# First attention, second half of the tokens: weights reloaded from DRAM as their stored high and low parts

## What is computed

```python
def _L0_xattn_ref(latents, context, Wq, Wk, Wv, Wo):
    H, KV, HD = (16, 4, 96)
    G = H // KV
    hidden = jnp.concatenate([context, latents], axis=1)
    q = (latents @ Wq.T).reshape(b, q_len, H, HD)
    k = (hidden @ Wk.T).reshape(b, s_len, KV, HD)
    v = (hidden @ Wv.T).reshape(b, s_len, KV, HD)
    ...
    attn = jax.nn.softmax(scores.astype(jnp.float32), axis=-1).astype(q.dtype)
    out = jnp.einsum('bkgqs,bksd->bkgqd', attn, v)
    return out @ Wo.T

x = x + _L0_xattn_ref(_layernorm(x, axis=-1), ctx_4096, ...)
x = x + _L0_ffn_ref(_layernorm(x, axis=-1), ...)
...
x = x + _L3_ffn_ref(_layernorm(x, axis=-1), L3_ffn_w1, L3_ffn_w2, L3_ffn_w3)
```

## Time and profile before

| | |
|---|---|
| median of 3 runs | 1762.42 us (1760.4 to 1762.99) |
| profiled execution | 1756.28 us |
| span of its trace | 1754.6 us |
| busy share PE, DVE, ACT, POOL | 83%, 64%, 26%, 18% |
| mean granted clock | 0.884 |
| read from and written to DRAM | 84.34 MB, 10.82 MB |

### The profile page before, as it was taken

How to read it: one execution, slowest core, us unless ns; L and a number is a source line. 1 busy time by engine, 2 the same in 40 slices (tenths; PEclk the granted TensorE clock), 3 DMA queues, 4 the chain that set the end, 5 groups by cost and what they waited for, 6 DMA issues and landing times.

```text
span 1754.6 us, 19242 instructions
## 1 busy us (share of the span) xinstructions
PE 1447.6 (83%) x6585; PEld 1148.8 (65%) x6585; DVE 1126.1 (64%) x2623; ACT 460.9 (26%) x994; POOL 312.5 (18%) x186
## 2 busy tenths in 40 slices
PE   6559999998999889898376878589997576589998
PEld 5337777775766668686265667377875465477786
DVE  4567777767767658767966656734466788854142
ACT  3223433433333323232212113113212322222010
POOL 4101211221112112111121013115422322012120
PEclk9889999999999989899655897569998778799999
DMA  5421331322223221331011012001111000001011
GB/s 187 152 70 51 89 87 49 97 72 72 69 66 84 65 61 42 84 82 41 24 43 38 25 49 90 17 1 36 52 46 48 24 1 1 0 24 61 13 38 48
DMA packets 99410, 96.43 MB, mean 55 GB/s; under 512 B 13138, under 2 KB 72418, under 8 KB 99314
## 3 DMA queue, kind: packets, MB, share of 16 engines
q1 hardware_dynamic: 98802, 94.35, 18.3%
q0 software_dynamic: 512, 0.85, 0.2%
HBM read 84.34 MB, written 10.82 MB: 54 GB/s over the span
## 4 chain that ended last, share of the span: by engine, by line
PE 62%; DVE 26%; issue 4%; ACT 4%; DMA 2%; SPq 1%; POOL 1%; DVEq 0%; ACTq 0%; POOLq 0%
PE bank L1651 48%; PE bank L1991 5%; PE bank L1743 4%; DVE nf_y L1595 3%; DVE st L1136 2%; DVE xn L1154 2%; PE bank L1676 1%; DMA nf_a<-in_L_w 1%; DVE mx L1504 1%; DVE e L1518 1%; PE bank L1733 1%; DVE sm L1516 1%; DVE xT L1113 1%; DVE mx L1187 1%; PE bank L1947 1%
## 5 line engine op out<-in xcount | busy, mean ns | idle before, releaser
L1651 PE MATMUL bank<-xT,slots 128*128 128x512 f32 (+1 forms) x1920 | 462.7, 399 | 9.7 <-DVE xT L1113 6.3
L808 POOL TENSOR_TENSOR slots<-staging,slots 128x1024 fp32r<-128x1024 f32 (+4 forms) x97 | 230.3, 2377 | 1112.3 <-ACT slots L896 1112.2
L1651 PEld LDWEIGHTS bank<-xT,slots 128*128 128x128 f32 (+1 forms) x1920 | 351.9, 184 | 107.7 <-issue 9.4
L1595 DVE TENSOR_SCALAR nf_y<-nf_w 128x512 fp32r<-128x512 f32 (+2 forms) x495 | 233.8, 499 | 25.3 <-PE bank L1991 24.3
L1651 PE MATMUL bank<-slots,h 128*128 128x512 f32 (+1 forms) x728 | 181.6, 410 | 20.1 <-DVE h L1243 13.9
L1651 PEld LDWEIGHTS bank<-slots,h 128*128 128x128 f32 (+1 forms) x728 | 142.9, 197 | 56.8 <-DVE h L1243 14.8
L1991 PE MATMUL bank<-nf_y,nf_d 128*128 128x512 f32 (+2 forms) x495 | 168.8, 425 | 11.3 <-DVE nf_y L1595 9.0
L896 ACT ACTIVATE slots<-staging 128x1024 fp32r<-128x1024 f32 (+4 forms) x97 | 98.1, 1018 | 187.8 <-PE bank L1651 173.7
L929 ACT ACTIVATE e<-bank,mx 128x320 f32<-128x320 f32 x128 | 66.3, 523 | 274.3 <-DVE mx L1190 270.3
L1209 DVE TENSOR_TENSOR x<-bank,x 128x512 f32<-128x512 f32 x72 | 49.7, 691 | 125.0 <-PE bank L1651 125.0
L1991 PEld LDWEIGHTS bank<-nf_y,nf_d 128*128 128x128 f32 (+1 forms) x495 | 94.2, 195 | 47.6 <-DVE nf_y L1595 16.9
(11 more groups left out here) (244 smaller groups left out, 1942.7 us busy)
## 6 DMA issues: line engine op xcount, KB each, us to landing
staging<-in_L_wqkT SPq DMA_DIRECT2D x16, 480.0 KB, 3.6
nf_out<-nf_w SPq DMA_DIRECT2D x30, 256.0 KB, 2.1
staging<-nf_out SPq DMA_DIRECT2D x30, 256.0 KB, 2.8
staging<-in_L_woT SPq DMA_DIRECT2D x16, 384.0 KB, 3.5
staging<-in_L_w SPq DMA_DIRECT2D x12, 512.0 KB, 4.0
nf_a<-nf_max SPq DMA_DIRECT2D x40, 128.0 KB, 3.6
nf_r<-nf_rcp SPq DMA_DIRECT2D x40, 128.0 KB, 3.5
nf_w<-in_L_w SPq DMA_DIRECT2D x15, 256.0 KB, 4.1
```

What stands on the lines that cost most here:

```text
L808: g.tensor_tensor(lo, split_source(i), hi.bitcast(FP32), ALU.subtract).then_inc(*sig.mark("weight_low", i))
L1595: v.tensor_scalar(nf_y[0:rows, i % STAIR_RING, 0:size], w_, bound, first, compare, ALU.mult)\
L1651: ins = mm(dst, l_, r_, start=i == 0, stop=i == len(passes) - 1)
```

## The change

`chunk` gets an argument `again`, the name of the first-half chunk with the same weights; the 18 second-half chunks carry it. For each of the 18 first-half chunks there is a DRAM tensor `saved`. After SP issues the load of the next but one staged chunk it also issues a DMA of the chunk's high and low parts from the ring slot to DRAM (960 KB for qk0, 768 KB for v0 and o0), after waiting for the save two before. A second-half chunk is no longer loaded to `staging` nor split by ACT and POOL. At the step where its split stood, SP waits for the slot to be free, for the save and for the reload two before, and issues one DMA of 960 or 768 KB from DRAM to the slot; PE waits for that DMA. The staging halves alternate over the staged chunks alone. A split into a slot whose former chunk was saved also waits for that save.

```diff
+        def chunk(name, p, dims, loads, dest=None, after=None, again=None):
...
+            if again is not None:
+                first_split[name] = again
+                saved[again] = dram(f"saved{len(saved)}", (p, 2, int(np.prod(dims))))
...
                 chunk(("v0", hf, i), P, (2, G0 * HD0), [((slice(None),), by_k(a["L0_wvT"], 2 * i, 2 * i + 2))],
                      again=("v0", 0, i) if hf else None)
...
+                      again=("qk0", s - G0, i) if s >= G0 else None)
...
+                      again=("o0", s - G0, i) if s >= G0 else None)
...
+            staged = [i for i in range(n_chunks) if chunks[i][0] not in first_split]
+            staged_before = {i: staged[n - 2] for n, i in enumerate(staged) if n >= 2}
...
                 for j in splits_here:
-                    while loads_here and loads_here[0] < j + 2:
+                    if chunks[j][0] in first_split:
+                        steps.append(("reload", j))
+                        continue
+                    while loads_here and (loads_here[0] <= j or staged_before.get(loads_here[0], -1) < j):
                         steps.append(("load", loads_here.pop(0)))
                     steps.append(("split", j))
...
+        def slot_free(engine, name):
+
+
+            n = slot_no[name]
+            if n >= NSLOT and known:
+                former = ring_names[n - NSLOT]
+                engine.wait_ge(*sig.when(*known.user["chunk", former]))
+                if former in saved:
+                    engine.wait_ge(*sig.when(f"weight_saved{save_no[former] % 2}", save_no[former]))
...
+                if n >= 2 and stage_names[n - 2] in saved:
+                    save_chunk(stage_names[n - 2])
+
+            def save_chunk(name):
+
+
+                _, p, dims, *_ = chunks[chunk_no[name]]
+                n = save_no[name]
+                if n >= 2:
+                    sp.wait_ge(*sig.when(f"weight_saved{n % 2}", n - 2))
+                sp.dma_start(saved[name], slots[0:p, slot_no[name] % NSLOT, :, 0:int(np.prod(dims))].bitcast(FP32))\
+                    .then_inc(*sig.mark(f"weight_saved{n % 2}", n, 16))
+
+            def reload_chunk(i):
+                name, p, dims, *_ = chunks[i]
+                n, k = reload_no[name], save_no[first_split[name]]
+                slot_free(sp, name)
+                sp.wait_ge(*sig.when(f"weight_saved{k % 2}", k))
+                if n >= 2:
+                    sp.wait_ge(*sig.when(f"weight_reloaded{n % 2}", n - 2))
+                sp.dma_start(slots[0:p, slot_no[name] % NSLOT, :, 0:int(np.prod(dims))].bitcast(FP32), saved[first_split[name]])\
+                    .then_inc(*sig.mark(f"weight_reloaded{n % 2}", n, 16))
...
             def split(i):
                 name, p, dims, loads, dest, after = chunks[i]
-                act.wait_ge(*sig.when(f"weight_staged{i % 2}", i))
-                if dest is None and slot_no[name] >= NSLOT and known:
-
-                    act.wait_ge(*sig.when(*known.user[("chunk", ring_names[slot_no[name] - NSLOT])]))
+                act.wait_ge(*sig.when(f"weight_staged{stage_no[name] % 2}", i))
+                if dest is None:
+                    slot_free(act, name)
...
             def need(name, user):
 
-                if known:
+                if known and name in first_split:
+                    n = reload_no[name]
+                    pe.wait_ge(*sig.when(f"weight_reloaded{n % 2}", n))
+                elif known:
                     pe.wait_ge(*sig.when("weight_low", chunk_no[name]))
```

More of the change, by code:

```diff
@@ L471, in build @@
         nf_out = [dram(f"nf_out{m}", (FT, P, D)) for m in range(3)]
-        chunks, chunk_no = [], {}
-        def chunk(name, p, dims, loads, dest=None, after=None):
+        chunks, chunk_no, first_split, saved = [], {}, {}, {}
+        def chunk(name, p, dims, loads, dest=None, after=None, again=None):
             chunk_no[name] = len(chunks)
             chunks.append((name, p, dims, loads, dest, after))
+            if again is not None:
+                first_split[name] = again
+                saved[again] = dram(f"saved{len(saved)}", (p, 2, int(np.prod(dims))))
         def by_k(ap, k0_, k1_):
@@ L495, in o0_chunks @@
                 rows = a["L0_woT"][(s % G0 * HPG + 2 * i) * HD0:(s % G0 * HPG + 2 * i + 2) * HD0]
-                chunk(("o0", s, i), HD0, (2, D), [((slice(None),), rows.rearrange("(h p) n -> p h n", p=HD0))])
+                chunk(("o0", s, i), HD0, (2, D), [((slice(None),), rows.rearrange("(h p) n -> p h n", p=HD0))],
+                      again=("o0", s - G0, i) if s >= G0 else None)
         v0_chunks(0)
@@ L643, in build @@
             n_chunks = len(chunks)
-            steps = [(kind, i) for i in range(n_chunks) for kind in ("load", "split")] + base
+            steps = [(kind, i) for i in range(n_chunks)
+                     for kind in (("reload",) if chunks[i][0] in first_split else ("load", "split"))] + base
         slot_no, n = {}, 0
@@ L651, in build @@
         ring_names = sorted(slot_no, key=slot_no.get)
+        stage_no = {n: i for i, n in enumerate(n for n in (c_[0] for c_ in chunks) if n not in first_split)}
+        stage_names = list(stage_no)
+        save_no = {n: i for i, n in enumerate(n for n in stage_names if n in saved)}
+        reload_no = {n: i for i, n in enumerate(n for n in (c_[0] for c_ in chunks) if n in first_split)}
+        def slot_free(engine, name):
[5 more added lines that the diff above has]
+                    engine.wait_ge(*sig.when(f"weight_saved{save_no[former] % 2}", save_no[former]))
         def flat(ap, dims):
@@ L775, in _ @@
                     load_chunk(*s[1:])
+                elif s[0] == "reload":
+                    reload_chunk(*s[1:])
                 elif s[0] == "nf_max":
@@ L785, in split_source @@
         def split_source(i):
-            _, p, dims, *_ = chunks[i]
-            return flat(staging[0:p, i % 2, 0:int(np.prod(dims))], dims)
+            name, p, dims, *_ = chunks[i]
+            return flat(staging[0:p, stage_no[name] % 2, 0:int(np.prod(dims))], dims)
         @block.gpsimd
@@ L2005, in _ @@
             for s in steps:
-                if s[0] in ("load", "split"):
+                if s[0] in ("load", "split", "reload"):
                     continue
```

20 lines of the change are left out of this document (12 added, 8 removed).

## The result

The changed kernel takes 1770.67 us (median of 6 runs, 1766.32 to 1774.25), the kernel before on the same chips 1762.74 us (6 runs, 1760.4 to 1766.63). The ratio is 1.0043 with a 95% interval of 1.0026 to 1.0060: slower, by some 8 us. The profiled execution took 1770.52 us with a span of 1768.7 us. The forecast was 1757.4 us and a gain of 5 us, so it had the wrong sign.

What follows compares the result with a forecast made beforehand. PE was taken as limited by POOL's work through DVE at the joints and by the DMA queue at the start. -16.4 + 10.35 + 1 = -5.05 us on 1762.42 gave 1757.4 us, range 1747 to 1769.

Steps and rivals of the forecast that it cites:

- Joints: Where stages meet: gain of 16.4 us, from closed PE gaps 11.9, the clock 3 and SP's freed waits 1.5.
- DVE's wait at an item's scales: At 580.8 us, 4.63 us behind SP's wait for an o0 split; gain counted 1.5 us, between 0 and 2.2.
- Start: Saves ahead of awaited row blocks on the DMA queue: loss of 10.35 us, bounds 5 and 16, passed whole to PE.
- four qk0 saves: Between 28 and 48 us: 11 us of transfers, less idle queue time, counted as a loss of 5.7 us.
- o0 saves ahead of the block awaited till 61.36 us: At the start: one o0 save of 2.2 us ahead of DVE's row block, 1.9 us of it lost.
- qk0 save ahead of the block awaited till 78.03 us: At the start: one save of 2.75 us ahead of DVE's row block, lost in full.
- the queue's idle time: Between 28 and 48 us: 3.9 us idle, set against 11 us of transfers, leaving 7.1 us.
- My upper bound: At the start: 16 us if all saves from 28 us on are paid in full (4 x 2.75 + 2.2 + 2.75).
- Middle: Rest of the first half: ten saves ahead of background stores and item loads, loss of 1 us, between 0 and 4.
- Reloads: Second-half chunks from DRAM: none late, 0 us, up to 2; tightest place had 14.7 us for 4.2 us.
- The first one: At the start, saves on the single DMA queue cost up to 20 us: +5 to +8 us, about 1769; chance 0.23.

Runs made afterwards that it cites:

- reloads alone: Changed kernel with all 18 reloads but only two chunks saved, which all reloads read (mostly wrong weights); 1750.24 us, ratio 0.9925 to the kernel before.
- POOL's part cut: Kernel before, with POOL's subtraction for the 18 second splits cut to the last 64, 192 or 256 columns; 1749.59 us, ratio 0.9916.
- saves alone: Changed kernel with the 18 saves issued, but second-half chunks loaded and split as before and nothing reloaded; 1785.7 us, ratio 1.0136 to the kernel before.
- fourteen: Changed kernel, saves behind four more row blocks, four early qk0 chunks not saved but split twice; 1755.86 us, ratio 0.9964 to the kernel before.
- eighteen saves put off: Changed kernel, each save behind four more row blocks or the next weight load, reload or turned block; 1753.73 us, ratio 0.9956 to the kernel before.
- nine saves: Changed kernel, only the nine chunks first split after 120 us saved and reloaded, the others split twice; 1763.16 us, ratio 1.0005 to the kernel before.

## Why the prediction was wrong

**Joints (forecast -16.4 us): right, perhaps a little high.** The seven gaps closed, in total -17.6 us by the offsets of one trace, -12 to -16 by the medians of the runs with reloads alone, with POOL's part cut, and of the changed kernel against the saves alone. One of the three terms was not there: DVE's wait at an item's scales, counted at 1.5 us, is 4.20 us instead of 4.63, and PE's gap behind it 2.94 instead of 2.18. What stands before those scales is the same in both kernels: SP needs some 12 us to issue the twenty small DMAs of that item (567.16 to 579.21 us before, 574.05 to 585.76 after). The cause of the gaps, POOL through DVE, is shown by cutting POOL's work alone.

**Start (forecast +10.35, bounds 5 to 16): the first step that failed, by size.** It is 16.8 us in the changed kernel's trace, 14.1 with the saves alone, whose steps at the start are the same. Its three terms, from the offsets of DVE's maxima at 48.73, 61.36 and 78.03 us before:

| term | forecast | changed kernel | saves alone |
|---|---|---|---|
| four qk0 saves, 28 to 48 us | 5.7 | 9.5 | 6.7 |
| o0 saves ahead of the block awaited till 61.36 us | 1.9 (one save) | 4.7 (two saves) | 5.0 (two saves) |
| qk0 save ahead of the block awaited till 78.03 us | 2.75 | 2.8 | 2.4 |

Two things were wrong in it. One is a count, and both traces show it: stage 0 has two o0 chunks, and the save of the first stands among the row blocks before the one awaited until 61.36 us. Two saves of 768 KB are 3.9 us at 403 GB/s, and 4.7 to 5.0 were lost where 1.9 were forecast. The other was to set the queue's idle time (3.8 us by the earlier trace rows; the prediction has 3.9), and more by following the blocks one by one, against the four qk0 saves. They are 9.8 us at 403 GB/s. The runs with fourteen and with eighteen saves put off differ by 8.4 us at the statistics, the traces above show 9.5 and 6.7, so 0.3 to 3.1 us of the idle time were of use, not 3.9 and more. An account that fits, argued and not shown: the queue is idle there because the loop of four blocks waits for DVE, and a block that lands late behind a save frees its buffer late, so that the next load starts late. The third place, where nothing was set off, came out as forecast. My upper bound, every save in full, would have been 18.2 us with the seventh save in it. I took 10.35, near the middle of the bounds, where the runs lie at 14.1 and 16.8.

**Middle (forecast +1, bounds 0 to 4): the second step that failed, and by as much.** It is 7.2 us in the changed kernel, 9.3 with the saves alone and 9.3 with nine saves; 6 to 8 us of the miss are here, 4 to 6 at the start. Here the mechanism was wrong, not only the size. I argued that PE has projections to cover DVE's late start on an item. At the item traced above they did not: its comparisons feed PE one by one, PE's steps stand in a fixed order, and the late item opened four gaps of 0.2 to 1.2 us, with the lower clock behind them. I had looked for gaps over 1 us. That the saves' place on SP's queue is the cause is shown by putting them off (1 us lost instead of 9.3); that every item loses in the way of the one traced is not.

**Reloads (forecast 0): right.** At the tightest place, behind the last v0 product at 377.00 us, the reloads are issued at 379.27 and 379.9 us; of those near there the slowest lands after 8.7 us. The first use is at 393.88 us. The profile shows one wait of PE for a reload, 0.4 us.

**The rivals.** The first one, that the start costs more than the joints give, had the sign and the figure (+5 to +8 us, about 1769), at a chance of 0.23. The figure is in part luck. Its mechanism at the start, the single queue, is what moving the saves to another queue (10 us less there) and behind the blocks (8 us less) show. But it put the loss at the start alone, at 20 us and with a threshold of 19; in fact it was 14.1 to 16.8 at the start and 7.2 to 9.3 in the middle, where another queue did not help. The weight it got was too small for a reason that the prediction itself names: 23.0 us of waits at the very place where the saves were to be added.

## What to carry to other kernels

Where an engine already waits for blocks from a DMA queue, count the bytes put ahead of them nearly in full (here 14.1 to 16.8 us for 16.1 us of transfer), and be slow to set idle time of the queue against it. A transfer that nobody waits for belongs behind the ones that somebody does; here up to four steps of order were worth 15 to 17 us, about what the reloads themselves won. A wait that grew by 1.4 us on an engine that feeds TensorE through many short steps cost a series of short gaps and then a lower clock, so look for the sum of small gaps and the granted clock, not for long gaps alone. And a trace is one execution: what two of them differ by far from the change is to be held against the spread of the timed runs.

## What the runs showed of the hardware

- Loads behind saves on one queue: the row blocks' median to landing rose from 3.7 to 5.4 us (256 KB, tile `nf_a`; from 4.1 to 5.1 for `nf_w`), and SP itself was held: issuing two blocks took 4.23 us in place of 0.9.
- With the same saves on ACT's queue the row blocks landed in 3.7 us (`nf_a`) and 4.3 (`nf_w`), nearly as before, and the start lost 6.8 us instead of 16.8. The saves themselves gained little: at the start 960 KB landed in 6.4 us there and 6.5 on SP's queue, over the whole kernel in 4.6 and 6.3, and 768 KB in 5.6 and 6.0.
- The loss at the start was in proportion to the bytes, 14.1 us for 6.5 MB and 7.1 us for half of it; the fixed part comes out at 0.2 us, known to some 4 us.
- Shortening POOL's subtraction shortened DVE's comparisons from a mean of 543 to 448 ns and the kernel by 13 to 15 us, with the same instructions in the same order on both engines.
